# Row maxima of a 16-head attention: products over each head's own 64 rows, in pairs

## The reference

```python
q = (x1 @ wq.T).reshape(b, n, HEADS, HEAD_DIM).transpose(0, 2, 1, 3)
k = (x2 @ wk.T).reshape(b, m, HEADS, HEAD_DIM).transpose(0, 2, 1, 3)
v = (x2 @ wv.T).reshape(b, m, HEADS, HEAD_DIM).transpose(0, 2, 1, 3)
dots = jnp.einsum('bhnd,bhmd->bhnm', q, k) * SCALE
attn = jax.nn.softmax(dots, axis=-1)
out = jnp.einsum('bhnm,bhmd->bhnd', attn, v)
...
return out @ wo.T + bo
```

## Time and profile before

| | us |
|---|---|
| median of three runs | 544.36 |
| lowest, highest | 538.31, 545.44 |
| span of the profiled execution | 534.7 |
| TensorE products busy | 500.6 |
| TensorE weight loads busy | 335.8 |
| VectorE busy | 276.7 |
| ScalarE busy | 187.7 |
| POOL busy | 161.2 |

### The profile page before, as it was taken

The page is one execution under the profiler, slowest core; times in us unless marked ns, Lnnn a source line. Parts: engine busy times, 40 slices in busy tenths (PEclk is TensorE's granted clock), DMA queues, the critical chain, the costliest instruction groups (busy, mean ns, idle before and its releaser), DMA issues.

```text
span 534.7 us, 9480 instructions
## 1 busy us (share of the span) xinstructions
PE 500.6 (94%) x3452; PEld 335.8 (63%) x3452; DVE 276.7 (52%) x664; ACT 187.7 (35%) x444; POOL 161.2 (30%) x180
## 2 busy tenths in 40 slices
PE   9989898999998969999999988899999899999991
PEld 8556654454566657788877767787866575444441
DVE  3466651221227475656676877988654226223352
ACT  2343231211114345555555564556662104200000
POOL 3130123011126044332231562543201467100242
PEclk9999999999999998999999999999999999999997
DMA  5999994499877697885664209400000153111100
GB/s 138 265 277 313 385 348 127 158 361 392 310 244 219 147 252 170 209 234 139 173 163 97 54 1 331 143 2 3 1 1 1 42 150 113 41 37 54 27 12 24
DMA packets 52588, 82.33 MB, mean 154 GB/s; under 512 B 10910, under 2 KB 41126, under 8 KB 52541
## 3 DMA queue, kind: packets, MB, share of 16 engines
q1 hardware_dynamic: 45788, 69.05, 43.5%
q0 software_dynamic: 5776, 12.13, 7.2%
q10 hardware_dynamic: 976, 0.53, 0.4%
HBM read 66.87 MB, written 15.15 MB: 153 GB/s over the span
## 4 chain that ended last, share of the span: by engine, by line
PE 78%; DVE 11%; issue 4%; DMA 2%; POOL 2%; ACT 2%; POOLq 0%; SPq 0%; DVEq 0%; ACTq 0%
PE pb L1551 72%; DVE hN L1111 1%; DVE nmx L1412 1%; POOL xs_dram L656 1%; DVE prob L1415 1%; PE pb L1990 1%; DMA hN<-yt_dram 1%; PE pb L1849 1%; PE pb L1759 1%; DVE ctxbuf L1342 1%; DVE nmx L1320 1%; PE pb L1561 1%; DVE x L1263 1%; PE pb L1723 1%; DMA xs_dram<-arena,slot 1%
## 5 line engine op out<-in xcount | busy, mean ns | idle before, releaser
L1551 PE MATMUL pb<-split 128*100 128x362 f32 (+2 forms) x320 | 77.3, 325 | 6.4 <-DVE nmx L1320 2.7
L1551 PE MATMUL pb<-ring,big 128*116 (+1 forms) x232 | 76.8, 578 | 0.0
L1320 DVE TENSOR_REDUCE nmx<-pb 100x1 f32<-100x361 f32 x128 | 62.7, 527 | 24.2 <-PE pb L1551 23.8
L1551 PEld LDWEIGHTS pb<-split 128*100 128x100 f32 (+2 forms) x320 | 54.7, 179 | 16.4 <-issue 5.7
L1551 PEld LDWEIGHTS pb<-ring,big 128*116 128x116 f32 (+1 forms) x232 | 31.2, 162 | 42.0 <-issue 40.9
L987 ACT ACTIVATE big<-pb 121x400 f32<-121x400 f32 (+1 forms) x96 | 48.1, 504 | 22.5 <-PE pb L1551 19.9
L721 POOL TENSOR_TENSOR shift<-consts,nmx 100x400 fp32r<-100x400 f32 x32 | 28.2, 882 | 77.6 <-DVE nmx L1320 77.5
L1551 PE MATMUL pb<-big,arena 121*32 121x100 f32 (+3 forms) x1072 | 47.9, 264 | 1.7 <-ACT arena L835 1.2
L1551 PEld LDWEIGHTS pb<-big,arena 121*32 121x32 f32 (+3 forms) x1072 | 29.1, 113 | 18.4 <-issue 6.9
L1551 PE MATMUL pb<-shift 100*121 100x400 f32 (+1 forms) x96 | 34.6, 361 | 0.0
L1551 PE MATMUL pb<-hT,wgu 128*128 128x400 f32 (+1 forms) x100 | 33.0, 469 | 1.3 <-DVE big L1205 1.0
(11 more groups left out here) (277 smaller groups left out, 839.7 us busy)
## 6 DMA issues: line engine op xcount, KB each, us to landing
ring<-in_L_ffn_gate_up_proj SPq DMA_DIRECT2D x12, 1024.0 KB, 9.5
split<-kx_dram SPq DMA_DIRECT2D x64, 181.0 KB, 4.1
ring<-in_L_ffn_down_proj SPq DMA_DIRECT2D x12, 512.0 KB, 7.6
kx_dram<-split POOLq DMA_DIRECT2D x16, 362.0 KB, 5.1
ctxbuf<-in_L_ffn_gate_up_proj SPq DMA_DIRECT2D x4, 1024.0 KB, 8.9
ring<-in_L_ffn_W_experts SPq DMA_DIRECT2D x4, 1024.0 KB, 12.7
ctxbuf<-in_ctxT SPq DMA_DIRECT2D x10, 361.0 KB
split<-qx_dram SPq DMA_DIRECT2D x64, 50.0 KB, 2.1
```

Source lines behind the costliest of these rows:

```text
L1320: nc.vector.tensor_reduce(nmx[:, t % 4, q:q + 1], PB[SB[n % 3]][0:T, 0:CTX], AX.X, ALU.max, negate=True) \
L1551: return nc.tensor.matmul(o, l, r, start=start, stop=stop)
```

## The change

`scores` takes rows 0 to 63 of both operands for an even head and rows 64 to 127 for an odd one, in place of all 128. The four products of a quad are no longer issued one each behind `j` = 0, 1, 2 and at the end of the thirds, but as two pairs: heads 0 and 1 behind `j` = 0, heads 2 and 3 behind `j` = 1. Banks, semaphores, operands in memory and all other engines' programs stay as they are.

```diff
@@ -1924,7 +1924,8 @@
                     pe.wait_ge(s(f"c_q4_{b % 2}"), 128 * (b // 2 + 1))
                 if n >= 3:
                     pe.wait_ge(s("c_max"), n - 2)
-                mm(PB[SB[n % 3]][0:T, 0:CEV], q4[:, b % 2, h % 2, h // 2, :], k4[b % 2][:, h // 2, :],
+                rows = slice(4 * DH * (h % 2), 4 * DH * (h % 2 + 1))
+                mm(PB[SB[n % 3]][0:T, 0:CEV], q4[rows, b % 2, h % 2, h // 2, :], k4[b % 2][rows, h // 2, :],
                    True, True).then_inc(s("c_s"), 1)
 
             def shifted_scores(t, j):
@@ -1959,10 +1960,9 @@
                         for w, b, i in bank6(t, "middle"):
                             bank6_part(w, b, i)
                     shifted_scores(t, j)
-                    if t + AHEAD < NQUAD:
-                        scores(4 * (t + AHEAD) + j)
-                if t + AHEAD < NQUAD:
-                    scores(4 * (t + AHEAD) + 3)
+                    if t + AHEAD < NQUAD and j < 2:
+                        scores(4 * (t + AHEAD) + 2 * j)
+                        scores(4 * (t + AHEAD) + 2 * j + 1)
                 if t >= 1:
                     weighted_values(t - 1)
                 for w, b, i in bank6(t, "end"):
```

## The result

The changed kernel takes 561.39 us (560.59 to 564.64, 4 runs) against 543.53 us before (4 runs): ratio 1.0381, 95% interval 1.0314 to 1.0448. Forecast: 559.7 us. So it is slower, by the size foreseen; but the sum had one term too few and one too large, and the clock brought one that the prediction didn't have.

The account below looks back on a forecast made before the run. TensorE was taken to bound the context attention: 0.48 us more in each of 30 turns is 14.4 us, plus 0.9 for late maxima, 15.3 on 544.36, giving 559.7 us. Its own range was 555 to 563 us, 8 in 10 548 to 567.

Parts of the forecast that it names:

- TensorE bounds the stage, so a turn's extra time is paid in full: Context attention, 188 to 322 us: TensorE's added time is paid in most of the stage, 0.48 us a turn.
- Cost of a change of shape: Around each 64-row pair: 0.10 us to enter, 0.11 to leave, weight load exposed; a pair costs 0.54 us instead of 0.34.
- The halves run at once: Within a pair: both 64-row products stream side by side, 0.17 us for the two.
- the rival of serial halves: Within a pair: the two halves stream one after the other, 6.6 us more, 566 us; chance 0.18.
- Head 3 waits for head 0's maximum: Second pair of a turn: three banks rotate, so head 3 streams at 1.02 us at the earliest, costing 0.08 us.
- The rival without drains: At each pair: 64 rows cause no drain, only head 3's wait remains; 4.5 us more, 548.9 us; chance 0.13.
- VectorE begins head 0's maximum late ... 3 x 0.3 = 0.9 us more: One quad of four: this maximum starts 0.67 instead of 0.37 us after its product; 0.9 us over three calm ones.
- No DMA, copy or POOL instruction is added or moved.: Other engines in the stage: nothing else is added or moved, and no time was added to the sum for it.
- The late quads put at 0: Four quads bounded by VectorE, near 276 and 311 us: savings and waits offset, 0 with -2 to +2 us.
- The signs: Profile after: about 0.25 us idle per pair, products 0.01 us apart, stage some 15 us longer, TensorE's busy share falling.
- The rival on the edit as mere order: All pairs: halves run as full-array products, so only the moved order counts; 549 us; chance 0.07.
- Packing pays: All 60 pairs: no drain and no binding wait for the maximum, 10.2 us less, 534 us; chance 0.05.

Follow-up runs that it names:

- e2: Kernel before with 64 rows in every product for the maximum, order unchanged: 562.04 us, ratio 1.0397.
- e7: Changed kernel with heads 2 and 3 issued behind the turn's middle piece, ahead of the third score group: 556.23 us, ratio 1.0272.
- e9: Kernel before, order unchanged, with 64 rows for heads 2 and 3 alone: 542.23 us, ratio 1.0013.
- e3: Changed kernel with heads 2 and 3 issued behind the third score group, ahead of the weighted values: 552.15 us, ratio 1.0184.
- e1: Changed kernel with all 128 rows again, pairs kept where the change puts them: 550.97 us, ratio 1.0175.
- e5: Changed kernel with all 128 rows in quads 0 to 7, 64 rows from quad 8 on: 553.79 us, ratio 1.0259.
- e10: The changed kernel run once more, unaltered, against the kernel before: 559.86 us, ratio 1.0341.
- e4: Changed kernel with heads 0 and 1 just ahead of the weighted values, heads 2 and 3 just behind them: 553.0 us, ratio 1.0231.
- e8: Both pairs beside the weighted values, and VectorE makes the late keys' low part ahead of the maxima of heads 0 and 1: 548.63 us, ratio 1.0155.
- e6: Changed kernel with 64 rows in quads 0 to 7 alone, all 128 from quad 8 on: 554.62 us, ratio 1.0245.

## Why the prediction was right, and where its sum was not

- **TensorE bounds the stage, so a turn's extra time is paid in full.** Right. The forecast said 0.48 us a turn; turns 9 and 11, calm ones without a late key piece, measured 0.49.
- **Cost of a change of shape.** Right, and for 64 rows too, which the rows of before didn't show: 0.11 us for entering, 0.10 for leaving (0.10 and 0.11 foreseen), with the load in the open. e2 puts a lone product's visit at 0.36 us over its 0.17 (0.53 - 0.17 foreseen), e7 two pairs at 0.39 (0.40 foreseen).
- **The halves run at once.** Right; the rival of serial halves falls. The speed of the pair itself, 0.17 us instead of 0.34, is real: e2's lone visit is as long as a pair's, and e9 and e3's second pair show the saved stream as what pays for an entry.
- **Head 3 waits for head 0's maximum.** Right: its product in the calm turns is issued 0.10 to 0.11 us behind head 2's (0.09 foreseen). The rival without drains leant on the same floor; it falls with the drains.
- **"VectorE begins head 0's maximum late ... 3 x 0.3 = 0.9 us more".** Over-sized: in turn 8 head 3 came 0.23 us behind head 2 instead of 0.10, 0.13 us each time, some 0.4 us in all. By the time TensorE got to head 3, 0.2 us later than in e1, most of the lateness had passed.
- **"No DMA, copy or POOL instruction is added or moved."** True as written, and the step that failed: it stands for a list of what may come late in which bank 6 is missing. No copy was moved in its own engine, but two TensorE products were taken from between the copy and the piece that waits for it. The missing term is 0.16 us in each turn with a late key piece, six of them between turns 7 and 19 and two before (turns 4 and 6), 1.3 us in all; e7 and e3 show its cause, since with a pair behind the middle piece the gap is 0.
- **The late quads put at 0.** Right: turns 19 to 31 lost 5.34 us, and the eleven of them that issue products give 5.3 at 0.48. That holds for their sum; single ones lie between -0.4 and +1.0 us.
- **The clock wasn't in the sum.** With 64 rows only from quad 8 on (e5) the first seven turns take 1.8 us more than before, in the changed kernel 9.6 and, again, 9.1. Six turns of shape changes are 6 x (0.60 - 0.30) = 1.8 of the difference; 5.5 to 6.0 us remain, and with them the stretch of 24 us at the lower level. (The clock took more of TensorE's time than that, some 8 us: the wait in turn 2, of 2.6 us in the kernel before and 3.0 in e5, is 0.8 in the changed kernel and 0.1 in e10, because TensorE gets there later, at 200.0 us instead of 196.9 in the changed kernel.) That is shown as a link between the rows of these products and the clock in one place of this kernel. Why it falls there isn't settled: the sandwiches (e4, e8) and e9 have 64-row products in the same turns, and 7 to 10 us at the lower level; the kernels in which 64-row products of the first turns are entered from the full array and left into it (after, e2, e3, e6, e7, e10) all have 24 to 27. That is what they have in common, and no run tests it alone.
- **The signs.** Idle time put to issue (13.9 us for 64 pairs, 0.22 each), the start of the two products within 0.01 us, head 3's wait and the maxima's 526 ns came as written. The stage grew by 22 us in the trace and not by 15, mostly by the clock, and TensorE's busy share in it didn't fall, because the waits lie inside of the products' records.

So at the full clock the stage lost about 1.8 + 1.8 + 7.2 + 5.3 = 16.1 us against 15.3 forecast, and the clock put 5.5 to 6 on top in the traces. The medians agree: e5 is 13.6 us over before, with its 1.8 us of missing shape changes 15.4, and the changed kernel 17.9 to 19.4. They leave less to the clock, 2.5 to 4 us, than the traces, since the executions of before have low stretches of their own (537.4 us at a clock of 0.987 to 545.4 us at 0.976), of which the profiled one has little. The forecast of 559.7 us stood on 544.36 us, the median of three runs, while the medians of the other jobs are 540.2 to 540.5: a base some 4 us too high and a cost some 4 us too low met in e10's 559.9 us. The mechanism and its price were right; that the number came within 2 us was in part luck.

The rival on the edit as mere order (0.12 us a turn and 0.9, so 4.5 us over before) describes e1, where the rows are full again. Its calm turns cost 0.14 us, but it is 9.5 to 11 us over before: the rival lacked bank 6 too. As an account of the changed kernel it falls, since the loads there have the open idle time that e1 doesn't have. "Packing pays" never came near: no kernel here beats the one before, and the best, e9, equals it.

## What to carry to other kernels

Packing two products into halves of the array saves one stream and costs an entry and an exit with a load in the open at each; with streams of 0.16 us that is 0.17 us gained for 0.37 paid. Pack where the shape changes anyway, or pack so many products per visit that the switches are small beside them. And when products are moved within an in-order engine, look at what used the time in which they ran: here it was a copy and a subtraction which freed a bank, and after the move they fell short of it by 0.16 us.

## What the runs showed of the hardware that was not expected

- Two 64-row loads of different halves take 0.16 us together, the same as one, and the two products begin in the same hundredth of a microsecond.
- An exit from the 64-row shape that leads into the 32-column shape costs no more than a change from the full array into that shape: 0.61 and 0.62 us between the same two instructions (e9 and before).
- TensorE's granted clock fell to its lower level for 24 to 27 us, with the engine busy by the records for 32.4 of 34 us, when the products of the stage's first turns had 64 rows (e6), and for 3.4 us when they had 128 rows (e5), which differs in nothing else in these turns. With 64 rows in other places of the turn (e4, e8, e9) it was 7 to 10 us. Busy time by the records didn't foretell the clock: 31.5 of 34 us at 0.65 in the changed kernel, 30.0 at 0.95 in the one before.
